# The first bilinear pass of an upsampling kernel: from TensorE matmuls to two GpSimd instructions over doubled loads

## The reference

```python
# layer 0
x = grouped_conv3x3_stride2(sx, w_down)            # (8, 256, 64, 64)
labels = kmeans(x[0])                              # channels of batch 0, 10 iterations
v5 = cluster_means(x, labels)                      # (8, 8, 64, 64)
mu, var = gmm_fit(v5)                              # 10 EM iterations
gate = sigmoid(...)                                # (8, 256)
pre_up = gate * x + x
up = repeat(pre_up, 2, axis=1) * w_up              # (8, 512, 64, 64)
y0, y1, fy = coords(64, 128)
rows = up[:, :, y0, :] * (1 - fy) + up[:, :, y1, :] * fy      # first bilinear pass
h = rows[:, :, :, x0] * (1 - fx) + rows[:, :, :, x1] * fx     # second bilinear pass
h = h + sx
# layer 1, on h (8, 512, 128, 128)
h = h + bias
u = fir_up2(h, up_filter)                          # 256x256, separable, 12 taps
u = leaky_relu(u, 0.2) * sqrt(2)
out = fir_down2(u, down_filter)                    # 128x128, separable
```

## Time and profile before

| what | value |
|---|---|
| median of 3 runs | 7448.8 us (7448.55 to 7449.44) |
| the profiled execution, its own time | 7447.51 us |
| its span in the profile | 7445.7 us |
| granted TensorE clock, mean | 0.967 |
| busy share PE / DVE / ACT / POOL | 94% / 80% / 61% / 34% |
| the chain that ended last, by engine | PE 79%, all others under 1% |
| resampling | from about 1522 us to the end |

### The profile page before, as it was taken

The page is one execution under the profiler, slowest core; times in us unless marked ns, Lnnn a source line. Parts: engine busy times, 40 slices in busy tenths (PEclk is TensorE's granted clock), DMA queues, the critical chain, the costliest instruction groups (busy, mean ns, idle before and its releaser), DMA issues.

```text
span 7445.7 us, 691936 instructions
## 1 busy us (share of the span) xinstructions
PE 6961.8 (94%) x302277; PEld 6350.0 (85%) x302277; DVE 5924.4 (80%) x11620; ACT 4571.4 (61%) x9038; POOL 2522.2 (34%) x3076
## 2 busy tenths in 40 slices
PE   6699994079999999999999999999999999999999
PEld 2444442069999999999999999999999999999998
DVE  7399998967777777777777777777777777777776
ACT  0100001347777777777777777777777777777776
POOL 0000000034444444444444444444444444444443
PEclk9699997589999999999999999999999999999999
DMA  6188883023333333333333333333333333333332
GB/s 262 47 320 321 320 319 134 0 69 96 99 96 98 96 98 97 98 96 98 97 97 97 97 97 97 97 97 98 97 98 96 98 96 98 96 99 96 99 96 82
DMA packets 1261249, 891.87 MB, mean 120 GB/s; under 512 B 184336, under 2 KB 1234960, under 8 KB 1244432
## 3 DMA queue, kind: packets, MB, share of 16 engines
q1 hardware_dynamic: 1249936, 856.58, 37.2%
q10 hardware_dynamic: 11264, 34.61, 1.7%
HBM read 587.94 MB, written 303.04 MB: 120 GB/s over the span
## 4 chain that ended last, share of the span: by engine, by line
PE 79%; issue 0%; DVE 0%; DMA 0%; POOL 0%; SPq 0%; ACT 0%; DVEq 0%; POOLq 0%
PE bank L1087 26%; PE bank L1082 25%; PE twin L1082 14%; PE twin L1087 13%; PE twin L1221 2%; DVE x_sum L1319 0%; DMA img<-in_x 0%; DVE leaky L1295 0%; DMA low<-conv_dram 0%; POOL img L1041 0%; DVE up L1304 0%; SPq L993 0%; ACT dn L1286 0%; SPq L994 0%; ACT res L1271 0%
## 5 line engine op out<-in xcount | busy, mean ns | idle before, releaser
L1295 DVE SCALAR_TENSOR_TENSOR leaky<-bank,slope_t 128x512 f32<-128x512 f32 x4096 | 2630.8, 683 | 909.8 <-ACT slope_t L1255 909.8
L1082 PE MATMUL bank<-up_t,up 64*64 64x133 f32 x65536 | 2757.6, 276 | 2.4 <-issue 1.5
L1087 PE MATMUL bank<-down_t,leaky 64*64 64x35 f32 (+1 forms) x131072 | 2295.9, 221 | 13.4 <-issue 11.4
L1087 PEld LDWEIGHTS bank<-down_t,leaky 64*64 64x64 f32 x131072 | 2260.6, 135 | 23.8 <-issue 15.0
L1255 ACT ACTIVATE slope_t<-bank 128x512 f32<-128x512 f32 x4096 | 2225.7, 599 | 1.9 <-PE bank L1082 1.9
L1082 PEld LDWEIGHTS bank<-up_t,up 64*64 64x64 f32 x65536 | 2026.9, 133 | 3.6 <-issue 3.5
L1050 POOL TENSOR_TENSOR low_d<-low_v 128x252 f32<-128x252 f32 x512 | 310.9, 607 | 4820.2 <-ACT low_v L1277 4820.2
L1319 DVE SCALAR_TENSOR_TENSOR x_sum<-lift,coef,img 128x128 f32<-128x128 f32 x4096 | 1439.7, 411 | 13.5 <-POOL img L1041 13.5
L1271 ACT ACTIVATE res<-twin 128x512 f32<-128x512 f32 x1024 | 612.0, 598 | 1326.8 <-PE twin L1087 1326.8
L1082 PE MATMUL twin<-up_t,x_sum 64*64 64x133 f32 x32768 | 1395.6, 281 | 7.2 <-DVE x_sum L1319 5.3
L1087 PE MATMUL twin<-down_t,dn 64*64 64x35 f32 (+1 forms) x65536 | 1364.0, 221 | 7.1 <-issue 6.8
(11 more groups left out here) (159 smaller groups left out, 1787.6 us busy)
## 6 DMA issues: line engine op xcount, KB each, us to landing
img<-in_x SPq DMA_DIRECT2D x1024, 256.0 KB, 2.9
out<-res SPq DMA_DIRECT2D x1024, 256.0 KB, 2.4
rows_next<-in_x SPq DMA_DIRECT2D x42, 4224.0 KB, 13.9
rows_next<-in_x SPq DMA_DIRECT2D x14, 4096.0 KB, 13.5
low<-conv_dram SPq DMA_DIRECT2D x1024, 32.0 KB, 2.2
conv_dram<-conv_next ACTq DMA_DIRECT2D x56, 512.0 KB, 4.1
rows_in<-in_x SPq DMA_DIRECT2D x6, 4224.0 KB, 14.0
rows_in<-in_x SPq DMA_DIRECT2D x2, 4096.0 KB, 29.7
```

Source lines behind the costliest of these rows:

```text
L1082: return pe.matmul(acc[cols(c), a:b], src[cols(rt), cols(c)], up_t[cols(rt), a:b], start=first, stop=False, skip_group_check=True)
L1087: return pe.matmul(acc[cols(c), a:b], src[cols(rt)], down_t[cols(rt), k, a:b], start=first, stop=False, skip_group_check=True)
L1295: v.scalar_tensor_tensor(out=leaky[1 - m % 2][:, e, i].rearrange("p k w -> p (k w)"), in0=u2_acc[e][i][:], scalar=GAIN, in1=slope_t[e][i][ ...
```

## The change

The matrix `lin` and its four matmuls go. In their place each of the 128 output rows (partitions) is brought the two input rows that it lies between: the near one, row p // 2, and the far one, above or below it. `low` grows to two such planes. A constant `beside` holds the two weights of every partition. POOL multiplies both planes by them in one instruction, in place (128x512), and adds them into `low_v` with a second (128x256); the rest of `widen` stays. ACT's copy to `low_v` goes, with the semaphores `b1_mm` and `b1_out` and PE's and ACT's waits for them. SP issues four DMAs per group instead of two, in the same place of its slot, and now waits until POOL has made the sum of the group before. POOL clears `low` once at the start. Apart from that, the convolution of batch 0 writes its tiles straight into `xx`, and the clustering no longer loads it.

```diff
-    parts["lin"] = np.concatenate([lin, lin])
+    near, far = p // 2, p // 2 - 1 + 2 * (p % 2)
+    inside = (far >= 0) & (far < HO)
+    beside = np.stack([lin[near, p], np.where(inside, lin[np.clip(far, 0, HO - 1), p], 0)], axis=1).astype(np.float32)
+    parts["beside"] = beside
...
-                conv = [sb(f"conv{i}", [P, QR, WO]) for i in range(2)]
+                tiles = [xx[:, n % CB, n // CB * QR * WO:(n // CB + 1) * QR * WO].rearrange("p (r w) -> p r w", r=QR) for n in range(UB)]
...
-                            dst = conv[n % 2][:, r0:V_ROWS, (1 if kw == 0 else 0):]
+                            dst = tiles[n][:, r0:V_ROWS, (1 if kw == 0 else 0):]
...
-                @block.sync
-                def _(sp):
-                    for cb in range(CB):
-                        sp.dma_start(xx[:, cb, :], conv_dram[cb * P:(cb + 1) * P]).then_inc(xx_loaded, 16)
...
-                    v.wait_ge(xx_loaded, 16 * CB)
...
-                low = sb("low", [P, 2, WO])
+                low = sb("low", [P, 2, LOWS, WO])
...
-                        done = cnt(u, r, m, 6, of=2)
+                        read = cnt(u, r, m, 6, per=LIFT, of=2) - (LIFT - 2)
...
-                            sp.wait_ge(b1_mm, done)
+                            sp.wait_ge(lift_step, read)
                         group = lows[:, bass.ds(g, LOWS), :] if u is None else lows[:, g:g + LOWS, :]
-                        sp.dma_start(low[0:HALF], group[:, 0:2]).then_inc(low_loaded, 16)
-                        sp.dma_start(low[HALF:P], group[:, 2:4]).then_inc(low_loaded, 16)
+                        for t in range(2):
+                            sp.dma_start(low[t:P:2, 0], group).then_inc(near_loaded, 16)
+
+                        sp.dma_start(low[1:P - 1:2, 1], group[1:HO]).then_inc(far_loaded, 16)
+                        sp.dma_start(low[2:P:2, 1], group[0:HO - 1]).then_inc(far_loaded, 16)
...
+                    nc.gpsimd.memset(low[:], 0.0).then_inc(low_cleared, 1)
...
                         if after(u, 0):
 
                             pool.wait_ge(x_summed, cnt(u, r, m, 2))
-                        pool.wait_ge(b1_out, cnt(u, r, m, 6, of=2))
+                        pool.wait_ge(near_loaded, cnt(u, r, m, 6, per=32, of=2))
+                        pool.wait_ge(far_loaded, cnt(u, r, m, 6, per=32, of=2))
+                        nc.gpsimd.tensor_tensor(low[:].rearrange("p s c w -> p s (c w)"), low[:].rearrange("p s c w -> p s (c w)"),
+                                                const("beside")[:, :, None].to_broadcast([P, 2, LOWS * WO]), ALU.mult).then_inc(lift_step, 1)
+                        pool.wait_ge(lift_step, step + 1)
...
+                        nc.gpsimd.tensor_tensor(low_v[:], low[:, 0], low[:, 1], ALU.add).then_inc(lift_step, 1)
+                        pool.wait_ge(lift_step, step + 2)
                         nc.gpsimd.tensor_tensor(low_d[:], low_v[:, :, 1:WO], low_v[:, :, 0:WO - 1], ALU.subtract).then_inc(lift_step, 1)
...
-                        if group:
-                            n_low = n_of(u, r, m, 6, per=32, of=2)
-                            pe.wait_ge(ready, FILTERS)
-                            pe.wait_ge(low_loaded, n_low)
...
-                            for c in range(2):
-                                for rt in range(2):
-                                    mm = pe.matmul(b1_acc[rt][cols(c)], const("lin")[cols(rt), cols(c)],
-                                                   low[cols(rt)].rearrange("p c w -> p (c w)"),
-                                                   start=not has(u, 3), stop=False, skip_group_check=True)
-                            mm.then_inc(b1_mm, 1)
...
-                        if m % 2 == 0 and has(u, -4):
-                            act.wait_ge(b1_mm, cnt(u, r, m, 6, of=2))
...
-                            nc.scalar.activation(low_v[:].rearrange("p (i c) w -> p i (c w)", i=2), twin[:, :, D2:D2 + 2 * WO], ACT.Copy).then_inc(b1_out, 1)
```

More of the change, by code:

```diff
@@ L69, in constants @@
     lin[i1, np.arange(H)] += f
-    parts["lin"] = np.concatenate([lin, lin])
+    near, far = p // 2, p // 2 - 1 + 2 * (p % 2)
+    inside = (far >= 0) & (far < HO)
+    beside = np.stack([lin[near, p], np.where(inside, lin[np.clip(far, 0, HO - 1), p], 0)], axis=1).astype(np.float32)
+    assert ((lin != 0).sum(axis=0) == (beside != 0).sum(axis=1)).all()
+    parts["beside"] = beside
     assert (i0[1:-1] == np.repeat(np.arange(HO - 1), 2)).all() and f[0] == f[-1] == 0 and i0[-1] == HO - 1
@@ L160, in first_convolution @@
                 rows_in = [sb(f"rows_in{i}", [P, 2, IN_ROWS, W]) for i in range(2)]
-                conv = [sb(f"conv{i}", [P, QR, WO]) for i in range(2)]
+                tiles = [xx[:, n % CB, n // CB * QR * WO:(n // CB + 1) * QR * WO].rearrange("p (r w) -> p r w", r=QR) for n in range(UB)]
                 in_loaded = [sem(f"in_loaded{i}") for i in range(2)]
-                conv_stored = [sem(f"conv_stored{i}") for i in range(2)]
+                conv_stored = sem("conv_stored")
                 vec_step = sem("vec_step")
@@ L251, in _ @@
                         act.wait_ge(t_done, n + 1)
-                        if n >= 2:
-                            act.wait_ge(conv_stored[n % 2], 16 * (n // 2))
-                        nc.scalar.activation(conv[n % 2][:, V_ROWS:, :].rearrange("p r w -> p (r w)"),
+                        nc.scalar.activation(tiles[n][:, V_ROWS:, :].rearrange("p r w -> p (r w)"),
                                              bank[n % 2][:, 0:T_ROWS * WO], ACT.Copy).then_inc(t_copied, 1)
@@ L258, in _ @@
                         act.dma_start(conv_dram[cb * P:(cb + 1) * P, q * QR * WO:(q + 1) * QR * WO],
-                                      conv[n % 2][:].rearrange("p r w -> p (r w)")).then_inc(conv_stored[n % 2], 16)
-                    for i in range(2):
-                        act.wait_ge(conv_stored[i], 16 * UB // 2)
+                                      tiles[n].rearrange("p r w -> p (r w)")).then_inc(conv_stored, 16)
+                    act.wait_ge(conv_stored, 16 * UB)
         def other_convolutions(sohp, xx):
@@ L460, in clusters @@
                 padded = sem("padded")
-                xx_loaded = sem("xx_loaded")
                 step = sem("step")
@@ L941, in resample @@
                 D2 = 2 * W
-                b1_acc = [bank[i][:, D2:D2 + 2 * WO] for i in range(2)]
                 images = x.rearrange("b c h w -> h (b c) w")
@@ L947, in resample @@
                 PAIRS = UNITS // 2
+                LIFT = 5
                 FIRST, LAST = -4, PAIRS + 2
@@ L1021, in slot @@
                             store(u, r, m)
+                    sp.wait_ge(low_cleared, 1)
                     for u in range(-6, FIRST):
@@ L1045, in widen @@
                         dst = lift[(m // 2) % 2]
+                        step = cnt(u, r, m, 4, per=LIFT, of=2)
                         if after(u, 0):
                             pool.wait_ge(x_summed, cnt(u, r, m, 2))
-                        pool.wait_ge(b1_out, cnt(u, r, m, 6, of=2))
+                        pool.wait_ge(near_loaded, cnt(u, r, m, 6, per=32, of=2))
[3 more added lines that the diff above has]
+                        pool.wait_ge(lift_step, step + 1)
+                        if after(u, -2):
+                            pool.wait_ge(lifted, cnt(u, r, m, 4, of=2))
+                        nc.gpsimd.tensor_tensor(low_v[:], low[:, 0], low[:, 1], ALU.add).then_inc(lift_step, 1)
+                        pool.wait_ge(lift_step, step + 2)
                         nc.gpsimd.tensor_tensor(low_d[:], low_v[:, :, 1:WO], low_v[:, :, 0:WO - 1], ALU.subtract).then_inc(lift_step, 1)
                         nc.gpsimd.tensor_copy(dst[:, :, 0:W:W - 1], low_v[:, :, 0:WO:WO - 1]).then_inc(lift_step, 1)
-                        pool.wait_ge(lift_step, cnt(u, r, m, 4, per=3, of=2) + 1)
+                        pool.wait_ge(lift_step, step + 3)
                         nc.gpsimd.tensor_tensor(low_f[:], low_d[:, :, :, None].to_broadcast([P, LOWS, WO - 1, 2]), weights,
                                                 ALU.mult).then_inc(lift_step, 1)
-                        pool.wait_ge(lift_step, cnt(u, r, m, 4, per=3, of=2) + 3)
+                        pool.wait_ge(lift_step, step + LIFT)
                         nc.gpsimd.tensor_tensor(dst[:, :, 1:W - 1].rearrange("p c (w t) -> p c w t", t=2), low_f[:],
@@ L1151, in begin_up @@
                                 n_res = n_of(u, r, m, -3)
-                            if m % 2 == 1:
-                                n_b1 = n_of(u, r, m, 5, of=2) if has(u, -3) else PAIRS // 2
                             pe.wait_ge(ready, FILTERS)
@@ L1179, in slot @@
                     def slot(u, r, m):
-                        group = m % 2 == 0 and has(u, -4)
                         p = m % 2
@@ L1228, in slot @@
                             n_half = n_of(u, r, m, -2)
-                            if group:
-                                n_b1 = n_of(u, r, m, 6, of=2)
```

(2 more changed lines are left out.)

25 lines of the change are left out of this document (6 added, 19 removed).

## The result

The changed kernel takes 7627.5 us (median of 4 runs, 7623.9 to 7628.3) against 7449.1 of the kernel before on the same chip: 178 us more, a ratio of 1.0237 with a 95% interval of 1.0219 to 1.0255. Slower was forecast, but by 70 us, and 7627.5 lies 17 us above the upper end of the range.

The account below looks back on a forecast made before the run. PE was taken to bound the kernel at 11.45 us per group; afterwards DVE and POOL would set 11.61. 7447.5 + 82 (512 x 0.16) - 12 for `xx` gives 7517.5, forecast as a 7519 us median, range 7308 to 7610.

Parts of the forecast that it names:

- What bounds the kernel now: Resampling, before the change: PE's order sets the time, 11.45 us per group; other engines count only by making PE wait.
- the block: First bilinear pass on PE: its removal saves 0.24 us per group, 123 us, if PE still sets the time.
- the loss of ACT's copy: ACT's copy to `low_v`, 0.38 us per group: hidden between others, so nothing gained except as POOL's release.
- How x_sum and POOL meet: DVE's x_sum waits for a running POOL instruction, passes one of its four, then POOL's next ready one goes first.
- Where POOL's freed work lands: `lift` and the bias addition hold even x_sum, 2.4 us instead of 1.13; DVE and POOL set the period, 11.61 us.
- half one: From the end of odd x_sum through POOL's chain to the end of even x_sum: 6.6 us.
- Half two: From the end of even x_sum through image load and bias addition to odd x_sum's end: 4.9 or 5.1 us.
- The clustering: DVE's wait for `xx` before the minimum, 12.5 us, goes: 12 us less.
- SP and the loads: Four low DMAs instead of two hold SP 3.3 instead of 1.6 us in the even slot: hidden, no cost.
- rival 3: SP's low DMAs issued over 1.03 us apart delay the image load: much slower, near 8280 at double price; chance 0.08.
- The range: Whole kernel's time: 7308 to 7610 us, meant to leave out no more than 2 in 10.
- Rival 1: Resampling: PE stays the bound, the full 0.24 us per group is kept, 7314 us; chance 0.22.

Follow-up runs that it names:

- run 2: Changed kernel with POOL's odd bias addition waiting for the even x_sum, `low_f` and `lift` moved behind it, and waits moved forward: 7304.5 us, ratio 0.9806.
- run 5: Changed kernel without POOL's multiplication, `low` going unweighted into the addition: 7304.3 us, ratio 0.9802.
- run 9: Kernel before without the first pass's four matmuls and the loads of `low`, ACT's copy kept: 7370.1 us, ratio 0.9889.
- run 1: Changed kernel with POOL's odd-slot bias addition also waiting until the even slot's x_sum is done: 7365.2 us, ratio 0.9887.
- run 3: Changed kernel with only POOL's waits moved: former `lift` to the front, loads ahead of x_sum: 7562.7 us, ratio 1.0151.
- run 10: Changed kernel with POOL's addition over 252 columns instead of 256 and `low_v` cleared at the start: 7651.7 us, ratio 1.0268.
- run 6: Kernel before with only batch 0's convolution writing straight into `xx` and the load of `xx` gone: 7435.5 us, ratio 0.9981.
- run 4: Changed kernel without its two far-row DMAs and POOL's wait for them: 7631.5 us, ratio 1.0245.
- run 7: Kernel before with one full matmul of the four of the first bilinear pass: 7464.5 us, ratio 1.0019.
- run 8: Kernel before with the first pass's four matmuls cut to one of 4 columns: 7447.0 us, ratio 0.9992.

## Why the prediction was right in kind and wrong in size

*What bounds the kernel now*: right in the main. PE's order sets the time before, and PE's own period without the pass is 11.19 us (runs 2 and 5), where 11.21 was said. That the two agree is partly luck: the block was worth 0.22 and not 0.24 (run 9), and the loss of ACT's copy, which the prediction put at nothing, some 0.07 more.

*How x_sum and POOL meet*: right, and run 1 shows it. The alternation read from the start of resampling, one x_sum instruction between two of POOL's, is there in every group. The first x_sum instruction of the even slot waits for the rest of `lift` (4013.96 to 4014.86, 0.90), and, what cost the time, a second POOL instruction gets in before the second of x_sum. The Trainium skill's rule (SBUF — State Buffer, Who interferes with whom), an exclusive lock per instruction, agrees with it.

*Where POOL's freed work lands*: right, down to x_sum starting in `lift` and the bias addition behind it. But this is the step that failed, in its size: the length of POOL's chain from the odd x_sum to `lift`, a term of half one. Half one was laid out as 6.6 us and measured 6.96: the multiplication starts 0.23 after x_sum instead of 0.07 (+0.16), the gap before the addition is 0.16 instead of 0.08 (+0.08), the addition takes 0.73 instead of 0.61 (+0.12). These three are 0.36, all of it. Half two was 4.9 to 5.1, 5.01 in the forecast's 11.61, and measured 4.83 here and 4.86 on average, which hid a part of the error. Together 11.83 and not 11.61, and 512 x 0.22 = 113 us is the miss of 108. I had priced `widen`'s added waits at nothing, by a row where the wait that came last was also the last of its row, and the addition by an instruction of nearly the same size. Run 3 shows that two of the three terms go when the waits are moved; run 10 shows that the third isn't from the length of the addition's runs, and what it is from stays open.

*The clustering*: 12 us, right (run 6, and 174.74 to 162.61 for the minimum's start is 12.1 in the traces).

*SP and the loads*: priced at nothing, right (run 4). The four issues stand at most 0.97 apart in this group (4001.79, 4002.76), under the 1.03 of rival 3, whose sum gives 6.7 and not the 6.8 written there.

*The range*: its upper end had room for 0.04 us per group over the layout's own 11.75, too little. I had written that the prices of two instructions never seen could add 0.2 each way, which is 102 us on 7590, and then took 20 of it. Rival 1, PE staying the bound, did not happen in the changed kernel, but it is what runs 2 and 5 reach, at 7304 where 7314 was worked out.

## What to carry to other kernels

When an engine is let go earlier, ask what it will then run beside: its late release may be what keeps two engines out of each other's way, and here the same instructions in another order are worth 323 us. On a circle through two engines the waits have a price too, and it was worth 65 us here to put those that are already satisfied in front of the one that is late. And when a profile says that an engine is busy throughout, compare starts with starts: in run 1 PE was busy for 1998 of 2000 us and still waited 0.11 us per group.

## What the runs showed of the hardware

- A VectorE instruction with two SBUF operands (x_sum) waits for the end of a running GpSimd instruction that reads SBUF, and then a GpSimd instruction that is ready goes ahead of the second x_sum instruction: 1.08 and 1.12 us for the first two instead of 0.34, in 422 of 422 groups (changed kernel; run 1 takes the second hold by the bias addition away).
- Four matmuls of 64x64 on different quarters of the array take 0.25 us as a block on average, one takes 0.22, and one of 4 columns 0.21; with the block behind them that is 0.70, 0.70 and 0.69, against 0.48 without any (runs 7, 8, 9).
- The multiplication on POOL starts 0.08 us after the x_sum that releases it when that wait is the last of a row (runs 2, 3), 0.17 with one satisfied wait behind it (run 4) and 0.23 with two (changed kernel); in run 5 the addition, with three, starts 0.31 after it. It isn't the number of waits alone: in run 10 two gave 0.23 and 0.33 in turn.
- POOL's 128x256 addition of two halves of one tile takes 0.73 us, its 128x252 subtraction of shifted columns 0.61; with the addition at 252 columns it is still 0.72 (run 10). The reason is open.
